# Moving the early slots' table from the last batch but one into the last batch, in a fused attention and mixture-of-experts kernel

## The reference

```python
# layer 1, per batch entry; relu attention, 16 heads of 16, causal
out = _layernorm(x, g1, b1) @ (sf_w * mask).T + sf_b;   x = x + out
x = x + _attention(_layernorm(x, g2, b2), ...)          # relu(scores)*causal / (sum + 1e-9)
x = x + relu(_layernorm(x, g3, b3) @ ff1_w.T + ff1_b) @ ff2_w.T + ff2_b
x = _layernorm(x_in + x)
# layer 2, over all 4096 tokens
aff = x @ centroids.T;  assign = argmax(aff, axis=1)    # one expert of 8 for each token
alpha = sigmoid(aff[assign])
h = relu(_layernorm(x, ln_g[e], ln_b[e]) @ w1[e].T + b1[e])
y = x + h @ w2[e].T + b2[e]
out = alpha * y + (1 - alpha) * x
x = _layernorm(x + out)
```

## Time and profile before

| what | value |
|---|---|
| median of three timed runs | 823.2 us |
| the profiled execution, its own time | 821.07 us |
| its span, from first to last instruction | 819.3 us |
| granted clock of TensorE, mean | 0.997 |
| busy: PE, DVE, ACT, POOL | 98%, 70%, 44%, 35% of the span |
| chain that ended last, by engine | PE 91%, DVE 6%, the rest 3% |

### The profile page before, as it was taken

One profiled execution on the slowest core, in us unless ns is written; L12 is line 12 of the kernel. 1 busy time (PEld: TensorE's weight loads), 2 busy tenths in 40 slices (PEclk: granted clock), 3 DMA queues, 4 the chain that ended last, 5 costly groups with the idle time before them and its releaser, 6 DMA issues.

```text
span 819.3 us, 19058 instructions
## 1 busy us (share of the span) xinstructions
PE 800.8 (98%) x7042; PEld 540.1 (66%) x7042; DVE 573.0 (70%) x1608; ACT 360.7 (44%) x603; POOL 286.9 (35%) x419
## 2 busy tenths in 40 slices
PE   9999999999999999999999999999999999999995
PEld 6654575476466467557557546859989977877674
DVE  6665398789779869779789965624579566666573
ACT  2444426424534532642642552232323376657761
POOL 4504011431512503313233051315455445443432
PEclk9999999999999999999999999999999999999998
DMA  7801020130040020021011033224543898788950
GB/s 266 264 2 26 7 73 1 54 78 0 28 105 1 26 54 1 3 71 58 1 54 53 5 106 129 111 70 160 190 152 126 289 345 310 272 323 314 338 225 17
DMA packets 63954, 96.43 MB, mean 118 GB/s; under 512 B 39347, under 2 KB 52276, under 8 KB 55926
## 3 DMA queue, kind: packets, MB, share of 16 engines
q1 hardware_dynamic: 58566, 83.56, 30.3%
q0 software_dynamic: 4864, 11.10, 4.2%
q10 hardware_dynamic: 432, 0.54, 0.2%
HBM read 84.22 MB, written 11.23 MB: 116 GB/s over the span
## 4 chain that ended last, share of the span: by engine, by line
PE 91%; DVE 6%; issue 1%; ACT 1%; another core or an unknown queue 0%; POOL 0%; POOLq 0%; DVEq 0%; ACTq 0%
PE ps L699 14%; PE ps L706 13%; PE ps L808 10%; PE ps L827 10%; PE ps L633 9%; PE ps L657 8%; PE ps L860 4%; PE ps L844 4%; PE ps L603 4%; PE ps L507 3%; PE ps L550 3%; PE ps L665 3%; PE ps L557 3%; PE ps L794 1%; DVE r2xhT L1220 1%
## 5 line engine op out<-in xcount | busy, mean ns | idle before, releaser
L706 PE MATMUL ps<-ff2T,hT 128*128 128x256 f32 x512 | 119.6, 385 | 0.2 <-ACT hT L1744 0.2
L699 PE MATMUL ps<-x3x,ff1T 128*128 128x512 f32 x256 | 118.2, 605 | 0.1
L1752 ACT ACTIVATE arena<-ps 128x1536 f32<-128x1536 f32 (+3 forms) x49 | 65.1, 1328 | 103.3 <-DVE arena L1149 102.6
L706 PEld LDWEIGHTS ps<-ff2T,hT 128*128 128x128 f32 x512 | 94.7, 190 | 21.8 <-issue 8.6
L827 PE MATMUL ps<-w_sb,arena 128*128 x400 | 95.8, 382 | 0.0
L1970 POOL TENSOR_TENSOR rs_ln<-mv_ln,eps 128x4 f32<-128x4 f32 x23 | 4.7, 203 | 259.9 <-DVE mv_ln L998 259.9
L699 PEld LDWEIGHTS ps<-x3x,ff1T 128*128 128x128 f32 x256 | 46.0, 189 | 59.0 <-issue 50.9
L1149 DVE SCALAR_TENSOR_TENSOR arena<-ps,arena 128x512 f32<-128x512 f32 (+4 forms) x59 | 45.1, 771 | 51.7 <-PE ps L657 34.2
L827 PEld LDWEIGHTS ps<-w_sb,arena 128*128 128x128 f32 x400 | 72.2, 190 | 12.4 <-issue 4.6
L633 PE MATMUL ps<-arena 32*128 32x512 f32 (+7 forms) x896 | 73.0, 434 | 1.8 <-ACT hT L1168 1.4
L1744 ACT ACTIVATE hT<-ps,col 128x512 f32<-128x512 f32 x64 | 43.1, 683 | 51.3 <-PE ps L699 51.3
(11 more groups left out here) (249 smaller groups left out, 1533.6 us busy)
## 6 DMA issues: line engine op xcount, KB each, us to landing
arena<-in_w SPq DMA_DIRECT2D x27, 1024.0 KB
hT<-in_w SPq DMA_DIRECT2D x16, 1024.0 KB
wts<-in_w SPq DMA_DIRECT2D x9, 1024.0 KB
w_sb<-in_w SPq DMA_DIRECT2D x8, 1024.0 KB, 5.6
token_store<-x SPq DMA_DIRECT2D x8, 520.0 KB, 3.3
w_sb<-in_x SPq DMA_DIRECT2D x48, 64.0 KB, 2.4
arena<-in_x SPq DMA_DIRECT2D x6, 512.0 KB, 4.0
arena<-in_epack SPq DMA_DIRECT2D x18, 134.0 KB
```

Source lines behind the costliest of these rows:

```text
L699: last = eng.matmul(ps[:, 6 + m % 2, :], ff1T[:, kd, m * P:(m + 1) * P], xT3[:, kd, :], start=kd == 0, stop=kd == KD - 1)
L706: last = eng.matmul(quarter(bank, half), hT[:, m, t * P:(t + 1) * P], ff2T[:, m, :], start=m == 0, stop=m == FM - 1)
L1752: eng.activation(o, i, ACT.Relu).then_inc(s_sa, 1)
```

## The change

The table for the early slots was worked out in pass 6, in steps 6, 7 and 8. It is now worked out in pass 7: the count of tiles in step 2, behind `dve_values`, and all the rest in step 5, behind the masking of that step's scores and ahead of the two `dve_turn_out`, `dve_affinity` and the context's first turn. The statistics of the slots 0 and 1 go from step 6 to step 7, and their normalisation from step 7 to step 8, behind `dve_add_ffn`. No instruction is added, removed or altered, and the order on PE, ACT, POOL and SP is the same.

```diff
@@ -1567,6 +1567,13 @@
                     dve_ln3_T(eng, f)
                 if n == 3 and b == 0:
                     dve_ln2(eng, 1)
+                if not more and n == 2:
+
+                    dve_count_tiles(eng, 0)
+                if not more and n == 5:
+                    dve_place_tiles(eng, 0)
+                    dve_find_experts(eng, 0)
+                    dve_slot_table(eng, 0)
                 if n == 5:
                     dve_turn_out(eng, b, 0)
                     dve_turn_out(eng, b, 1)
@@ -1579,21 +1586,12 @@
                     dve_add_ffn(eng, f, 0)
                 if n == 8 and not more:
                     dve_add_ffn(eng, f, 0)
-                if g == N_CUT - 1:
-
-                    if n == 6:
-                        dve_count_tiles(eng, 0)
+                if not more:
+
                     if n == 7:
-                        dve_place_tiles(eng, 0)
-                        dve_find_experts(eng, 0)
-                    if n == 8:
-                        dve_slot_table(eng, 0)
-                if not more:
-
-                    if n == 6:
                         slot_dve_in_stats(eng, 0)
                         slot_dve_in_stats(eng, 1)
-                    if n == 7:
+                    if n == 8:
                         slot_dve_in_norm(eng, 0)
                         slot_dve_in_norm(eng, 1)
             if more and b:
```

## The result

| | median of the timed runs | ratio to before, 95% interval |
|---|---|---|
| before | 822.99 us (821.58 to 823.41) | |
| changed | 825.59 us (824.42 to 827.05) | 1.0035 (1.0026 to 1.0044) |

What follows compares the result with a forecast made beforehand. PE, busy for 98% of the span, was taken as the bound. -1.69 - 2.29 + 1.4 = -2.6 us on the profiled 821.07 us gave 818.5, or 820.6 us timed with 2.1 us carried over; range 819.4 to 823.4.

Steps and rivals of the forecast that it cites:

- Pass 6, -1.69 us: Pass 6 without the table becomes as long as pass 5, saving PE 1.69 us.
- The count in step 2: Step 2 of pass 7: the count's 1.85 us fit into DVE's 2.16 us idle ahead of step 3's scores, cost 0.
- The wait ahead of unit 6, +1.4 us: Step 5 of pass 7: the rest of the table delays L1278, so PE waits 1.4 us ahead of unit 6.
- The loss of 2.29 us, -2.29: Step 5 of pass 7: PE's 2.29 us loss vanishes as the small transfers beside it move later.
- the burst: Small transfers of the first slots, SP's constant packs and POOL's gathers, at 484 to 490 us; said to slow PE 2.29 us.
- rival 1: The loss moves with the burst to step 7's weighing matmuls, again 2.29 us: -0.3 us in all, 822.9 us; chance 0.20.
- The later arrival of the transfers: Gathers, packs and early weights come later but keep their cover ahead of slot 0, cost 0.
- Rival 3: The burst, stretched to about 12 us, costs 4.6 us in two places: +2.0 us, 825.2 us, slower; chance 0.08.

Runs made afterwards that it cites:

- count6: Changed kernel with the count of tiles back in pass 6, step 6: 815.68 us against 815.93 before; repeated on an 823 chip, 821.84 against 822.32.
- count_split: Changed kernel, step 2 keeping only the count's parts that POOL does not hold, copy made a reduction, rest in step 5: 822.62 us against 822.58 before.
- all_step5: Changed kernel with the whole table, count included, in step 5 of pass 7: 823.92 us against 822.58 before.
- forms: Kernel before with three reductions and one test instruction, of another form each pass, added in step 2 of passes 2 to 5: executed once, 823.1 us.
- after_third: Changed kernel, unaltered, run again on an 816 chip: 820.13 us against 815.98 before.
- stats_later: Kernel before with only the statistics and normalisation of slots 0 and 1 a step later: 815.93 us against 815.93 before.
- after_again: Changed kernel, unaltered, run again on another 823 chip: 825.12 us against 822.58 before.

## Why the prediction was wrong, step by step

- **Pass 6, -1.69 us: right.** 65.80 us, no wait ahead of L550.
- **The count in step 2, costed at 0: this step failed.** "1.85 us fit into them" took the durations of pass 6 to a place where POOL adds 128x1024 numbers twice. Two of its instructions were held for 1.99 and 1.95 us, and PE waited 2.24 us ahead of step 4. `count6`, `count_split`, `all_step5` and `forms` show it: the held forms and the place together. Taking the held instructions out of this place gives 2.5 to 4.4 us back, and still 1.2 us where the whole count then stands on PE's path (`all_step5`).
- **The wait ahead of unit 6, +1.4 us: right in kind and nearly in size** where nothing else is late (1.24 us in `count6`). In the changed kernel it was 1.96 us, as DVE was behind from step 3 on.
- **Not in the sum at all: the clock.** Behind waits of 1.92 to 2.24 us the clock fell in four of seven cases, at 1.7 us of stretched matmuls behind unit 6 (5.40 instead of 3.70 us) or 1.55 behind step 4. All three profiles of the changed kernel have one fall.
- **The loss of 2.29 us, -2.29: half right.** It was tied to the burst and left step 5, but it did not vanish. In the versions that move the burst it came back as 1.6 to 1.8 us of PE one or two steps later, which is what rival 1 says. I gave that 0.20 and should have given it more: nothing in the profile spoke for its vanishing. In the first profile of the changed kernel PE waits only 0.20 us ahead of step 7, for there the slower clock had already made PE late: its scores of step 6 were done at 499.40 and masked from 500.16, 1.11 us behind the last gather. On 816 chips the loss does not exist, and the change costs more.
- **The later arrival of the transfers at 0: right.** Rows of slots 0 and 1 were there in time. The normalisation ended at 513.8 us, ahead of L794 at 517.0.

For the first profile the start times give the sum: -1.34 us at L550 (pass 6, less 0.3 us by which this execution was late from its start); +2.23 up to L657 of step 5, for the wait ahead of step 4; -2.29 up to unit 5; and +4.19 from there to L794. The last is 2.1 us of later start of unit 6, 1.7 us of clock, and 0.4 us in what follows. Together +2.79 us. For `after_third` against `stats_later` they are -1.6, +2.2 and 1.55 (wait and clock in step 4), and 1.5 at unit 6, and this makes 3.7 of the measured 4.2 us. Rival 3, the case slower than before, came near the measured time, but by a burst that costs more, and this is not what happened.

What stays open: by what way the gathers reach PE on the 823 chips, and why not on the 816 chips; why PE's signal comes late while its rows do not; and what decides whether the clock falls behind a wait.

## What to carry to other kernels

A gap on an engine is worth its length only to instructions that nothing in it can hold. Before a small instruction of DVE is put into one, look at POOL's timeline there, and at the instruction's form: beside a large addition of POOL a copy, a tensor_scalar or a tensor_tensor of two SBUF tensors of eight numbers cost 1.75 to 1.99 us, a reduction 0.2 to 0.4 us. When work is moved to shorten one pass, put it behind the instruction for which the busiest engine waits, not ahead of it; here this made -1.7 and -1.8 us out of -0.5 and -0.3 us.

## What the runs showed of the hardware

- **A hold does not need a large instruction on DVE.** Eight numbers on one partition waited for POOL's 1024 on 128, to within 0.02 us of its end.
- **The loss on the 823 chips ends with the gathers.** L1149 of step 6, or PE's next matmuls, started 0.81 to 1.13 us behind the last of POOL's four gathers in nine profiles; on 816 chips, with the same gathers, L1149 started ahead of their end.
- **The clock and waits.** Behind PE's waits of 1.24 us it never fell (`count6`, `count6_2`, `after_again`, `after_third`), nor behind those of 1.62 to 1.72 us ahead of step 7. Behind 2.24 us it fell in two of five profiles, behind 1.92 and 1.96 us in both, and behind 3.18 us not. The length of the wait alone doesn't decide. Behind a fall the clock was at 1.2 GHz for some 3 to 3.5 us.
- **Two kinds of chips.** The kernel before takes 816 us on some and 822 to 823 us on others, with the same instructions and a mean granted clock of 0.995 to 0.997 on both. The profiled executions of before and of `stats_later` are 5.5 us apart in span; 2.3 of these lie in step 5 of pass 7, and the rest in short stretches of the second layer. Each chip was used once, so that it is the chip and not the time of use isn't shown.
